# A transformer layer on eight cores: x transposed on the host and read with plain loads, its row-order copy cast by a separate DMA

## The chip, the cores and the metric

One Trainium2 chip, all eight cores. Each core runs the same program on one batch element of the input (4096 rows of 1024), so no core talks to another. The time is device microseconds of the slowest core. The kernel before takes 2436.91 us, the median of three runs.

## What is computed

The reference, cut to what matters, for one batch element:

```python
qkv = x @ W_qkv + b_qkv                       # x: [4096, 1024]
q, k, v = jnp.split(qkv, 3, axis=-1)
attn = jax.nn.softmax(q @ k.T / 32, axis=-1)
h = _layernorm(x + (attn @ v) @ W_out + b_out)
# feed-forward: groups of 16 rows, 64 expert slots; each slot takes one row of each group
perm = (logits == logits.max(over the 16 rows))
inter = relu(sel @ f1 + bias) @ f2
y = _layernorm(h + scatter(inter, perm))
```

x is needed twice: with its 1024 features on the partitions, as the moving operand of the projections, and in row order, as the residual that is added after the attention.

## The kernel before, in words

It is written engine by engine: a helper records an instruction for one engine (line 116 for every DMA, 121 for every wait, 127 and 130 for matmuls, 137 and 139 for ACT and DVE), and every wait is written by hand. The order of the program text is the order on each engine. Semaphores are counted per channel; a DMA adds 16 to its channel when it has landed.

Start. The GpSimd queue (POOL, queue q0 of the profile) casts DRAM to DRAM and DRAM to SBUF in this order: x rows 0 to 511 into the bf16 scratch xbf (channel xq0), the eight 128-row slabs of the Q weights (wc0 to wc7), x rows 512 to 1023 (xq1), eight slabs of K weights, x rows 1024 to 2047 (xq2), eight slabs of V weights, x rows 2048 to 4095 (xq3). All these 28 DMAs are issued at once; nothing waits on POOL.

Projections (Q, K, V). Eight blocks b of 512 rows. SyncE (SP, queue q1) waits for the piece of x that holds the block and for block b-2 to be done (two buffers), then issues eight transposing DMAs that put the block, features on partitions, into arena A. TensorE waits for all eight. Then, in order of the block: Q, eight groups m of eight 128x512 matmuls, banks m%4; K, the same; V, eight groups, banks 4 to 7. ScalarE (ACT) takes each Q group out of PSUM into one of two 512-column slots of the tile qstage and issues its DMA to the DRAM scratch qsp on its own queue (q10). Before it writes a slot it waits until the former DMA out of that slot, that of group m-2, has landed. The K groups also pass through ACT, into arena B; the V groups through VectorE (DVE), into arena C. The wait for the slot stands on ACT, in order, so K's evictions stand behind it; a bank of Q or K is free once ACT has taken it out, and V stands behind K on TensorE.

```python
wait("sync", xq_chan(b), 16)
wait("sync", "sT", xblk_T[buf])
for c in range(NCH):
    xv = dma("sync", xchan, A[:, xoff + c * 512: xoff + (c + 1) * 512],
             xbf_d[b * 512:(b + 1) * 512, c * 128:(c + 1) * 128],
             transpose=True)
```

```python
slot = m % 2
qchan = "qs%d" % slot
wait("scalar", qchan, P_cnt[qchan])      # the former write out of this slot
```

Attention. When the last projection is done, POOL loads the output weights and casts f1 and f2 (16 MB of fp32 each) DRAM to DRAM into bf16 scratch, eight DMAs in a row. SP loads the first two tiles of Q from qsp and, per 256 rows of queries, two 128-row tiles of xbf as the residual. Sixteen query tiles follow, each with 32 key tiles; then the routing logits, the gather of the selected rows, the expert matmuls, and the scatter with the second normalization. None of these stages is touched, but for the first load of the residual.

Of the kernel before, what the change touches and what calls it, by code (L numbers as in the profile page):

```python
# [8 lines left out]
F32 = mybir.dt.float32  # L9
BF16 = mybir.dt.bfloat16  # L10
# [3 lines left out]
D = 1024  # L14
# [7 lines left out]
def build_nc(S=4096, debug_scratch=False, stop_phase=99):  # L22
    nc = bass.Bass("TRN2", target_bir_lowering=False)
# [9 lines left out]
    SCR = "ExternalOutput" if debug_scratch else "Internal"  # L33

    x_d = nc.dram_tensor("x", [S, D], F32, kind="ExternalInput").ap()
    wqkv_d = nc.dram_tensor("wqkv", [D, 3 * D], F32, kind="ExternalInput").ap()
    bqkv_pc_d = nc.dram_tensor("bqkv_pc", [128, 16], F32, kind="ExternalInput").ap()
    bv_t_d = nc.dram_tensor("bv_t", [128, D], F32, kind="ExternalInput").ap()
# [10 lines left out]
    y_d = nc.dram_tensor("y", [S, D], F32, kind="ExternalOutput").ap()  # L49

    xbf_d = nc.dram_tensor("xbf", [S, D], BF16, kind=SCR).ap()
    qsp_d = nc.dram_tensor("qsp", [NCH, 128, S], BF16, kind=SCR).ap()
    hsp_d = nc.dram_tensor("hsp", [S, D], BF16, kind=SCR).ap()
    intersp_d = nc.dram_tensor("intersp", [ES, G, D], BF16, kind=SCR).ap()
# [23 lines left out]
          for i in range(8)]  # L78
# [27 lines left out]
    P_cnt = {s: 0 for s in CHANNELS + ["sT", "sV", "sC"]}  # L106
    P_ops = {e: [] for e in ENGINES}
    sems = {}
# [1 line left out]
    def op(eng, fn):  # L110
        P_ops[eng].append(fn)

    def dma(eng, chan, dst, src, **kw):
        P_cnt[chan] += 16
        op(eng, lambda e, d=dst, s=src, kw=kw, sm=chan:
           e.dma_start(d, s, **kw).then_inc(sems[sm], 16))  # L116
        return P_cnt[chan]

    def wait(eng, sname, v):
        if v and v > 0:  # L120
            op(eng, lambda e, sm=sname, vv=v: e.wait_ge(sems[sm], vv))

    def t_mm(out, lhsT, rhs, start, stop, inc=False):
        if inc:
            P_cnt["sT"] += 1
            op("tensor", lambda e, o=out, l=lhsT, r=rhs, st=start, sp=stop:
               e.matmul(o, l, r, start=st, stop=sp).then_inc(sems["sT"], 1))  # L127
        else:
            op("tensor", lambda e, o=out, l=lhsT, r=rhs, st=start, sp=stop:
               e.matmul(o, l, r, start=st, stop=sp))  # L130
        return P_cnt["sT"]
# [10 lines left out]
    def v_op(method, *args, inc=False, **kw):  # L142
        return eng_op("vector", "sV", method, *args, inc=inc, **kw)

    def c_op(method, *args, inc=False, **kw):
        return eng_op("scalar", "sC", method, *args, inc=inc, **kw)
# [20 lines left out]
    def xq_chan(b):  # L167
        row = b * 512
        for lo, hi, ch in xpieces:
            if lo <= row < hi:  # L170
                return ch
        return xpieces[-1][2]

    def emit_xpiece(i):
        if i < len(xpieces):
            lo, hi, ch = xpieces[i]
            dma("gpsimd", ch, xbf_d[lo:hi, :], x_d[lo:hi, :])

    emit_xpiece(0)
    for pi, (koff, pref) in enumerate(((0, "wc"), (1024, "wck"), (2048, "wcv"))):  # L180
        for k in range(NCH):
            dma("gpsimd", "%s%d" % (pref, k),
                A[:, k * 3072 + koff: k * 3072 + koff + 1024],
                wqkv_d[k * 128:(k + 1) * 128, koff:koff + 1024])
        emit_xpiece(pi + 1)
    dma("sync", "sm", BQ[:], bqkv_pc_d)
    dma("sync", "sm", GLM[:], glmask_d)
    dma("sync", "sm", IDT[:], ident_d)
# [10 lines left out]
    for b in range(NB):  # L199
        buf = b % 2  # L200
        xoff = XB0 + buf * 4096
        xchan = "xa%d" % buf
        wait("sync", xq_chan(b), 16)
        wait("sync", "sT", xblk_T[buf])
        xv = 0
        for c in range(NCH):
            xv = dma("sync", xchan, A[:, xoff + c * 512: xoff + (c + 1) * 512],
                     xbf_d[b * 512:(b + 1) * 512, c * 128:(c + 1) * 128],
                     transpose=True)

        wait("tensor", xchan, xv)

        for kind in ("Q", "K"):
            koff = 0 if kind == "Q" else 1024
            for m in range(NCH):
                pbi = m % 4
                sem, val = bank_free[pbi]
                wait("tensor", sem, val)
                tv = 0
                for k in range(NCH):  # L220
                    if b == 0 and m == 0:
                        wait("tensor",
                             ("wc%d" if kind == "Q" else "wck%d") % k, 16)
                    lhsT = A[:, k * 3072 + koff + m * 128:
                             k * 3072 + koff + m * 128 + 128]
                    rhs = A[:, xoff + k * 512: xoff + (k + 1) * 512]
                    tv = t_mm(pb[pbi][:], lhsT, rhs, k == 0, k == NCH - 1,
                              inc=(k == NCH - 1))
                wait("scalar", "sT", tv)
                wait("scalar", "sm", sm_done)  # L230
                if kind == "Q":
                    slot = m % 2
                    qchan = "qs%d" % slot
                    wait("scalar", qchan, P_cnt[qchan])
                    qsl = QS[:, slot * 512: slot * 512 + 512]
                    cv = c_op("activation", qsl, pb[pbi][:], AF.Identity,
                              inc=True, bias=BQ[:, m:m + 1])
                    wait("scalar", "sC", cv)
                    dma("scalar", qchan, qsp_d[m, :, b * 512:(b + 1) * 512], qsl)
                else:  # L240
                    cv = c_op("activation",
                              B[:, m * S + b * 512: m * S + (b + 1) * 512],
                              pb[pbi][:], AF.Identity, inc=True,
                              bias=BQ[:, 8 + m:8 + m + 1])
                bank_free[pbi] = ("sC", cv)

        wait("vector", "sV", init_v)
        wait("vector", "sm", sm_done)
        for sub in range(4):
            tt = b * 4 + sub  # L250
            for half in range(2):
                pbi = 4 + (sub * 2 + half) % 4
                sem, val = bank_free[pbi]
                wait("tensor", sem, val)
                tv = 0
                for k in range(NCH):
                    if b == 0 and sub == 0 and half == 0:
                        wait("tensor", "wcv%d" % k, 16)
                    lhsT = A[:, xoff + k * 512 + sub * 128:
                             xoff + k * 512 + sub * 128 + 128]  # L260
                    rhs = A[:, k * 3072 + 2048 + half * 512:
                            k * 3072 + 2048 + (half + 1) * 512]
                    tv = t_mm(pb[pbi][:], lhsT, rhs, k == 0, k == NCH - 1,
                              inc=(k == NCH - 1))
                wait("vector", "sT", tv)
                vv = v_op("tensor_tensor",
                          C_[:, tt * 1024 + half * 512: tt * 1024 + (half + 1) * 512],
                          pb[pbi][:], FP[:, half * 512:(half + 1) * 512],
                          ALU.add, inc=True)
                bank_free[pbi] = ("sV", vv)  # L270
        xblk_T[buf] = P_cnt["sT"]
# [48 lines left out]
    for qt in range(NQ):  # L320
# [6 lines left out]
            wait("tensor", sem, val)  # L327

        xrl_t = [0, 0]
        for sub in range(2):  # L330
            tt = qt * 2 + sub
            slot = tt % 2
            wait("sync", "sT", xres_free[slot])
            wait("sync", "h%d" % slot, h_spill[slot])
            xrl_t[slot] = dma("sync", "xr%d" % slot,
                              A[:, 15360 + slot * 1024: 15360 + (slot + 1) * 1024],
                              xbf_d[tt * 128:(tt + 1) * 128, :])
# [193 lines left out]
        while (ha_next + 1) * QC <= (qt + 1) * 256:  # L531
# [3 lines left out]
            for c in range(3):  # L535
# [3 lines left out]
                    transpose=True)  # L539
# [125 lines left out]
    for ec in range(4):  # L665
# [4 lines left out]
        for t in range(NT):  # L670
# [8 lines left out]
            for c in range(NCH):  # L679
                pbi = b0 + c // 4  # L680
                qtr = c % 4
                if qtr == 0:
# [8 lines left out]
                                                   c=NCH, e=16)  # L691
# [203 lines left out]
    for t in range(NT):  # L895
# [12 lines left out]
        for half in range(2):  # L908
            for c in range(4):
# [7 lines left out]
                      False, True, inc=True)  # L917
# [80 lines left out]
```

## Time and profile before

| | us |
|---|---|
| median of three runs | 2436.91 (2436.21 to 2487.02) |
| the profiled execution, its own time | 2434.68 |
| its span, slowest core (core 7) | 2433.1 |
| spans of the eight cores | 2405.8 to 2433.1 |
| TensorE busy in the span | 1932.8 |
| DMA bytes moved in the span | 230.62 MB |

The profile is of core 7. Its own time of 2434.68 us is 1.6 us above the span; the difference lies outside the first and the last instruction. In what follows, times on the axis are microseconds from the span's start. The DMA rows name queues: q0 is the one that POOL issues to, q1 that of SP, q10 that of ACT. A packet is the profile's unit, one contiguous run that one of the core's 16 DMA engines moves. Bytes of a cast are counted by its output.

### The profile page before, as it was taken

The page shows a single profiled execution, that of the slowest core. Times are in us where ns is not written, and L with a number is a line of the kernel's source. Part 1 is how long each engine was busy: PE and PEld are TensorE (multiplying, and loading weights), DVE is VectorE, ACT ScalarE, POOL GpSimd, SP SyncE. Part 2 cuts the span into 40 slices and gives each one's busy share as a digit, 9 for nine tenths or more (in the row PEclk, how much of TensorE's full clock was granted, in tenths as well). Part 3 has the DMA queues.
Part 4 walks back from the last instruction along what each step waited for, and adds up shares of the span by engine and source line. Part 5 has one row for each costly group of instructions (what it writes and reads, how often), then busy time and mean ns, then how long its engine had stood idle before and what let it go on. Part 6 is the DMA issues. An engine that isn't in the chain of part 4 may idle for free.

```text
span 2433.1 us, 36001 instructions; the slowest of 8 cores (2405.8 to 2433.1 us)
## 1 busy us (share of the span) xinstructions
PE 1932.8 (79%) x13216; PEld 1301.7 (54%) x13216; DVE 517.1 (21%) x840; ACT 555.9 (23%) x1121; POOL 127.4 (5%) x241
## 2 busy tenths in 40 slices
PE   0089999999399999999999999993567677665565
PEld 0034444478288777778877777881334343332222
DVE  0000101110110111111011111001514333432555
ACT  0023232222022222222222222220244333331000
POOL 2000000100000000000000000000011111112110
PEclk9999999999699999999999999996655655565777
DMA  9932131399600100001000100006265556556996
GB/s 131 120 62 61 38 67 44 71 116 115 107 10 18 40 27 27 27 19 31 19 27 27 40 27 23 6 19 136 70 176 183 165 181 170 175 164 196 314 311 234
DMA packets 234759, 230.62 MB, mean 95 GB/s; under 512 B 147488, under 2 KB 172064, under 8 KB 233760
## 3 DMA queue, kind: packets, MB, share of 16 engines
q0 software_dynamic: 21968, 84.03, 17.6%
q1 hardware_dynamic: 117904, 85.55, 13.9%
q10 hardware_dynamic: 94720, 58.74, 8.6%
q8 instruction: 114, 1.87, 0.3%
q14 instruction: 53, 0.43, 0.1%
HBM read 178.06 MB, written 92.27 MB: 111 GB/s over the span
## 4 chain that ended last, share of the span: by engine, by line
PE 63%; DMA 17%; another core or an unknown queue 7%; DVE 5%; issue 3%; ACT 2%; SPq 1%; DVEq 1%; ACTq 0%; POOL 0%; POOLq 0%
PE pb L130 55%; DMA intersp<-arenaB 8%; PE pb L127 8%; DMA arenaC<-hsp 4%; DMA arenaB<-intersp 2%; DMA y<-arenaF 2%; SPq L116 1%; DVE arenaB L137 1%; ACT arenaB L137 1%; DVE arenaA L137 1%; DMA arenaB<-f1b 1%; DVE bnbuf L139 1%; DVEq L139 1%; DVE arenaA L139 1%
## 5 line engine op out<-in xcount | busy, mean ns | idle before, releaser
L130 PE MATMUL pb<-arenaA,arenaB 128*128 128x256 bf16 (+1 forms) x4032 | 580.6, 288 | 63.6 <-DMA arenaA<-qsp 43.5
L130 PE MATMUL pb<-arenaA 128*128 128x512 bf16 x1856 | 457.7, 381 | 135.5 <-DMA arenaA<-xbf 133.0
L130 PE MATMUL pb<-arenaA,arenaC 128*128 128x256 bf16 x4120 | 540.0, 274 | 27.3 <-DVE arenaA L137 19.0
L130 PEld LDWEIGHTS pb<-arenaA,arenaB 128*128 128x128 bf16 (+1 forms) x4032 | 414.9, 105 | 170.2 <-issue 116.3
L130 PEld LDWEIGHTS pb<-arenaA,arenaC 128*128 128x128 bf16 x4120 | 402.3, 98 | 82.0 <-issue 34.7
L137 ACT ACTIVATE arenaA<-pb,smalls 128x256 bf16<-128x256 f32 x512 | 241.3, 474 | 796.7 <-PE pb L127 763.2
L130 PEld LDWEIGHTS pb<-arenaA 128*128 128x128 bf16 x1856 | 179.3, 98 | 364.8 <-issue 171.0
L130 PE MATMUL pb<-arenaB 128*128 128x512 bf16 (+1 forms) x384 | 164.1, 518 | 153.5 <-DVE arenaB L137 76.7
L139 DVE RECIPROCAL arenaF<-pb 128x256 f32<-128x256 f32 x16 | 28.1, 1758 | 881.8 <-PE pb L127 881.8
L130 PEld LDWEIGHTS pb<-arenaB 128*128 128x128 bf16 (+1 forms) x384 | 40.7, 112 | 266.6 <-issue 255.0
L127 PE MATMUL pb<-arenaA,arenaB 128*128 128x256 bf16 (+1 forms) x576 | 165.9, 288 | 0.0
L137 DVE CAST arenaB<-pb 128x512 bf16<-128x512 f32 x128 | 88.5, 692 | 272.5 <-DMA intersp<-arenaB 162.5
L130 PE MATMUL pb<-arenaC 128*128 128x128 bf16 x896 | 101.1, 282 | 51.8 <-DMA arenaC<-hsp 25.4
L127 PE MATMUL pb<-arenaA,ones_t 128*128 128x256 bf16 x512 | 139.6, 273 | 0.0
L137 DVE TENSOR_TENSOR arenaC<-pb,arenaF 128x512 bf16<-128x512 f32 x64 | 44.3, 692 | 422.2 <-PE pb L127 422.2
L130 PEld LDWEIGHTS pb<-arenaC 128*128 128x128 bf16 x896 | 79.1, 127 | 72.6 <-issue 71.7
L137 ACT ACTIVATE arenaB<-pb 128x512 bf16<-128x512 f32 x128 | 75.7, 596 | 161.3 <-DMA intersp<-arenaB 137.2
L139 DVE BATCH_NORM_STATS2 bnbuf<-pb 128x6 f32<-128x512 f32 x128 | 86.2, 694 | 112.5 <-PE pb L127 107.8
L116 POOL DMA_DIRECT2D intersp<-arenaB x128 | 69.2, 541 | 497.5 <-ACT arenaB L137 340.1
L139 ACT ACTIVATE bnbuf<-bnbuf,smalls 128x1 f32<-128x1 f32 x64 | 18.8, 294 | 327.2 <-DVE bnbuf L137 316.1
L137 ACT ACTIVATE arenaA<-pb 128x512 bf16<-128x512 f32 x128 | 76.4, 598 | 58.4 <-PE pb L127 58.1
L137 ACT ACTIVATE qstage<-pb,s_bqkv_pc 128x512 bf16<-128x512 f32 x64 | 44.0, 688 | 171.2 <-PE pb L127 125.9
(54 smaller groups left out, 944.6 us busy)
## 6 DMA issues: line engine op xcount, KB each, us to landing
arenaC<-hsp SPq DMA_DIRECT2D x128, 256.0 KB, 3.6
intersp<-arenaB POOLq DMA_DIRECT2D x128, 256.0 KB, 3.2
arenaB<-intersp SPq DMA_DIRECT2D x64, 256.0 KB, 16.3
arenaB<-intersp POOLq DMA_DIRECT2D x64, 256.0 KB, 9.2
y<-arenaF ACTq DMA_DIRECT2D x32, 512.0 KB, 9.6
qsp<-qstage ACTq DMA_DIRECT2D x64, 128.0 KB, 2.4
arenaA<-qsp SPq DMA_DIRECT2D x16, 512.0 KB, 3.9
arenaA<-xbf SPq DMA_DIRECT2D x32, 256.0 KB, 2.6
```

Of the source, the lines that this page charges most:

```text
L116: e.dma_start(d, s, **kw).then_inc(sems[sm], 16))
L127: e.matmul(o, l, r, start=st, stop=sp).then_inc(sems["sT"], 1))
L130: e.matmul(o, l, r, start=st, stop=sp))
L137: getattr(e, m)(*a, **k).then_inc(sems[sname], 1))
L139: op(eng, lambda e, a=args, k=kw, m=method: getattr(e, m)(*a, **k))
```

## The change

The host now also passes xt, the transpose of x, as a second fp32 input. The four pieces that POOL casts at the start are columns of xt, into a new scratch xbft, in place of rows of x into xbf. SP's 64 transposing DMAs become 64 plain DMAs of 128 rows by 512 columns out of xbft. xbf is still needed for the residual: one more DMA on POOL's queue, after the fourth piece, casts the whole of x, on a channel of its own (xbc), and SP waits for it ahead of the first residual load.

```diff
@@ emit_xpiece
             lo, hi, ch = xpieces[i]
-            dma("gpsimd", ch, xbf_d[lo:hi, :], x_d[lo:hi, :])
+            dma("gpsimd", ch, xbft_d[:, lo:hi], xt_d[:, lo:hi])
@@ start
         emit_xpiece(pi + 1)
+    xbc_done = dma("gpsimd", "xbc", xbf_d[:, :], x_d[:, :])
@@ projections, block b
             xv = dma("sync", xchan, A[:, xoff + c * 512: xoff + (c + 1) * 512],
-                     xbf_d[b * 512:(b + 1) * 512, c * 128:(c + 1) * 128],
-                     transpose=True)
+                     xbft_d[c * 128:(c + 1) * 128, b * 512:(b + 1) * 512])
@@ attention, query tile qt
         xrl_t = [0, 0]
+        if qt == 0:
+            wait("sync", "xbc", xbc_done)
@@ host
         m["x"] = np.ascontiguousarray(x[b])
+        m["xt"] = np.ascontiguousarray(x[b].T)
```

The queue of POOL at the start of the program, before. A DMA's shape is that of its destination in runs: 32x16384 is 32 contiguous runs of 16384 bf16 elements, 32 KB each.

```order
L116 DMA xbf<-x 32x16384
L116 DMA arenaA<-wqkv 128x1024 x8
L116 DMA xbf<-x 32x16384
L116 DMA arenaA<-wqkv 128x1024 x8
L116 DMA xbf<-x 64x16384
L116 DMA arenaA<-wqkv 128x1024 x8
L116 DMA xbf<-x 128x16384
L116 DMA arenaA<-wout 128x1024 [waits sT]
```

The same place in the changed program:

```order
L118 DMA xbft<-xt 1024x512
L118 DMA arenaA<-wqkv 128x1024 x8
L118 DMA xbft<-xt 1024x512
L118 DMA arenaA<-wqkv 128x1024 x8
L118 DMA xbft<-xt 1024x1024
L118 DMA arenaA<-wqkv 128x1024 x8
L118 DMA xbft<-xt 1024x2048
L118 DMA xbf<-x 256x16384
L118 DMA arenaA<-wout 128x1024 [waits sT]
```

The four pieces are now 1024 runs each, of 1, 1, 2 and 4 KB, and a DMA of 256 runs of 32 KB stands behind them. All else on the queue keeps its place.

SP's queue at the blocks 0 to 2, before:

```order
L116 DMA_TRANSPOSE arenaA<-xbf 128x512 [waits xq0]
L116 DMA_TRANSPOSE arenaA<-xbf 128x512 x7
L116 DMA_TRANSPOSE arenaA<-xbf 128x512 [waits xq1]
L116 DMA_TRANSPOSE arenaA<-xbf 128x512 x7
L116 DMA_TRANSPOSE arenaA<-xbf 128x512 [waits xq2,sT]
L116 DMA_TRANSPOSE arenaA<-xbf 128x512 x7
```

And in the changed program:

```order
L118 DMA arenaA<-xbft 128x512 [waits xq0]
L118 DMA arenaA<-xbft 128x512 x7
L118 DMA arenaA<-xbft 128x512 [waits xq1]
L118 DMA arenaA<-xbft 128x512 x7
L118 DMA arenaA<-xbft 128x512 [waits xq2,sT]
L118 DMA arenaA<-xbft 128x512 x7
```

The waits stay, the transposes become plain loads of 128 runs of 1 KB. ACT's queue is not changed; at the start it reads, the wait for the slot standing from the third group on:

```order
L137 ACTIVATE qstage<-pb,s_bqkv_pc 128x512 [waits sT,sm]
L116 DMA qsp<-qstage 128x512 [waits sC]
L137 ACTIVATE qstage<-pb,s_bqkv_pc 128x512 [waits sT,sm]
L116 DMA qsp<-qstage 128x512 [waits sC]
L137 ACTIVATE qstage<-pb,s_bqkv_pc 128x512 [waits sT,sm,qs0]
L116 DMA qsp<-qstage 128x512 [waits sC]
L137 ACTIVATE qstage<-pb,s_bqkv_pc 128x512 [waits sT,sm,qs1]
L116 DMA qsp<-qstage 128x512 [waits sC]
```

## Rows read from the trace of the kernel before

**Rows 1.** Groups of instructions, 0 to 467 us; busy, mean, idle before and releaser

```profile
L130 PE MATMUL pb<-arenaA 128*128 128x512 bf16 x1344 | 323.7, 381 | 133.0 <-DMA arenaA<-xbf 133.0
```

**Rows 2.** Timeline, 0 to 480 us: start, length, engine, what, idle before

```profile
15.82 123.98 SPq L116 DMA_TRANSPOSE arenaA<-xbf  x16
...
132.97 3.15 PE L130 MATMUL pb<-arenaA 128*128 128x512 bf16 x7 [132.97 <-DMA arenaA<-xbf]
...
136.33 2.47 PE L130 MATMUL pb<-arenaA 128*128 128x512 bf16 x7
...
138.85 1.67 PE L130 MATMUL pb<-arenaA 128*128 128x512 bf16 x7
...
466.70 0.38 PE L127 MATMUL pb<-arenaA 128*128 128x512 bf16 x1
```

**Rows 3.** Busy time by stretch: TensorE through one block, granted clock, DMA share

```profile
175.00:216.00 41.00, 41.00 (x192) 18.61 (x190) 5.53 (x8) 10.99 (x16) 0.00 (x0) 1.00 0.22 52
```

**Rows 4.** DMA issues of 0 to 17 us: KB each, us from issue to landing

```profile
xbf<-x POOLq DMA_DIRECT2D x1, 1024.0 KB, 14.2
...
arenaA<-wqkv POOLq DMA_DIRECT2D x8, 256.0 KB, 73.6
...
xbf<-x POOLq DMA_DIRECT2D x1, 4096.0 KB, 116.0
```

**Rows 5.** DMA queues, 44 to 52 us (packets, MB, share of 16 engines): weights against transposes

```profile
q0 software_dynamic: 588, 1.07, 91.5%
q1 hardware_dynamic: 588, 0.14, 14.9%
```

**Rows 6.** DMA queues, 100 to 120 us: the last piece of x against transposes

```profile
q0 software_dynamic: 65, 2.13, 92.0%
q1 hardware_dynamic: 68, 0.01, 0.6%
```

**Rows 7.** DMA queues, 105 to 115 us

```profile
q0 software_dynamic: 35, 1.15, 100.0%
```

**Rows 8.** DMA queues, 120 to 450 us: q10 carries the 64 writes of Q

```profile
q10 hardware_dynamic: 9216, 8.39, 9.3%
```

**Rows 9.** DMA queues, 540 to 620 us: the casts of f1 and f2 against plain DMAs

```profile
q0 software_dynamic: 322, 8.45, 96.4%
q10 hardware_dynamic: 258, 0.50, 1.6%
q1 hardware_dynamic: 306, 0.16, 1.3%
```

**Rows 10.** DMA issues of 500 to 620 us: the plain load of a Q tile

```profile
arenaA<-qsp SPq DMA_DIRECT2D x1, 512.0 KB, 108.9
```

**Rows 11.** DMA issues of 547 to 549 us: one write of ACT

```profile
hsp<-arenaA ACTq DMA_DIRECT2D x1, 256.0 KB, 43.4
```

**Rows 12.** Timeline of TensorE, 644 to 648 us

```profile
646.54 1.65 PE L130 MATMUL pb<-arenaA,arenaB 128*128 128x256 bf16 x7 [37.57 <-DMA arenaA<-qsp]
```

**Rows 13.** Timeline of ACT, 139 to 150 us: the wait for a slot of qstage

```profile
141.15 0.69 ACT L137 ACTIVATE qstage<-pb,s_bqkv_pc 128x512 bf16<-128x512 f32 x1 [1.21 <-DMA qsp<-qstage]
```

**Rows 14.** DMA queues, 1640 to 1680 us: 1024 runs of 128 bytes of the controller's cast

```profile
q0 software_dynamic: 1040, 0.13, 5.1%
```

**Rows 15.** Spans and granted clock of single cores

```profile
core 6: 2405.8 us, clock 0.877
core 7: 2433.1 us, clock 0.873
```

More of the change, by code:

```diff
@@ L35, in build_nc @@
     x_d = nc.dram_tensor("x", [S, D], F32, kind="ExternalInput").ap()
+    xt_d = nc.dram_tensor("xt", [D, S], F32, kind="ExternalInput").ap()
     wqkv_d = nc.dram_tensor("wqkv", [D, 3 * D], F32, kind="ExternalInput").ap()
@@ L51, in build_nc @@
     xbf_d = nc.dram_tensor("xbf", [S, D], BF16, kind=SCR).ap()
+    xbft_d = nc.dram_tensor("xbft", [D, S], BF16, kind=SCR).ap()
     qsp_d = nc.dram_tensor("qsp", [NCH, 128, S], BF16, kind=SCR).ap()
```

2 rows, old and new, of the table CHANNELS are left out of this document.

## The prediction

> **What bounds the kernel now.** I read the groups of instructions of the first 467 us, then the timeline around TensorE's first matmul, then the DMA queues stretch by stretch. TensorE's first matmul starts at 132.97 us, and the whole idle time is put down to the transposed loads of block 0 [rows 1, 2]. From there TensorE is never idle until the last projection at 467.1 us (466.70 + 0.38). In a clean block its 192 matmuls take 41.0 us by the window, and a group of eight starts every 1.72 us, so 24 groups are 41.3 us [rows 2, 3]. The granted clock is 1.00 there, that is 2.4 GHz.
>
> Why does block 0 arrive at 133 us when its piece of x has landed at 1.6 + 14.2 = 15.8 us [rows 4]? The queues tell it. From 44 to 52 us q0 moves 588 packets and q1 588; from 100 to 120 us, where q0's packets are 32 KB, 65 against 68 [rows 5, 6]. So the 16 DMA engines take one packet of q0 and one of q1 in turn, whatever their size. A packet of 32 KB takes 20 x 16 x 0.92 / 65 = 4.5 us, and each small packet of another queue waits for one. The transposes thus end with the last cast of x, which lands at 15.8 + 116.0 = 131.8 us [rows 4]. The same thing is seen later: from 540 to 620 us q0 casts f1 and f2 in 32 KB packets, 8.45 MB in 80 us; a plain load of 512 KB takes 108.9 us, a single ACT write 43.4 us, and TensorE stands idle for 37.57 us for that load [rows 9 to 12]. Plain DMAs starve as transposes do.
>
> Everything after 467 us (1966 us of the span) keeps its instructions, and its own flood of f1 and f2 starts with it. I cost it at no change. So the sum is about when the eighth block ends.
>
> **Removed: the transposes.** A plain load of 128 runs of 1 KB is 9 packets per engine, as the writes of Q show: 9216 / 64 / 16 = 9, the ninth being the semaphore's [rows 8]. A block is 8 x 8 = 64 data packets per engine. Beside the Q weights (2 KB packets, 0.915 x 8 x 16 / 588 = 0.20 us each [rows 5]) plus some 0.06 us for q1's own, 64 turns are about 17 us. Piece 0 lands near 16 us as before, so block 0 is there at about 33 us, and the Q weights with it. TensorE starts 100 us earlier. Alone this would be a gain of up to 100 us, less what the K and V weights hold back.
>
> **What is late next: the weights.** q0 goes in order. The V weights land about at 13.3 + 73.6 = 86.9 us for the median of the eight [rows 4]; the last one about 92 us, where the fourth piece must begin (4.19 MB at 2.13 MB per 20 us are 39 us before its landing at 131.8 [rows 4, 6]). I leave this as it is, since the bytes ahead of them are the same; transposes no longer take turns, but loads and writes do. Block 0 does Q and K meanwhile, waits, and ends its V part at 92 + 8 x 1.72 + 2 = about 108 us. Then SP may issue the load of block 2, and TensorE begins block 1, whose load has landed long before.
>
> **Added: the cast of the whole of x.** In the trace 8.45 MB in 32 KB packets take 80 us, and 1.15 MB 10 us, so 8.39 MB are 73 to 79 us [rows 7, 9]; I take 76. It stands behind the fourth piece, which I leave at 132 us (64 packets of 4 KB per engine at (132 - 92) / 64 = 0.6 us). So the new DMA runs from 132 to 208 us, with 256 / 16 = 16 packets per engine, 4.7 us each. During it every other queue gets 16 packets per engine, and no more. Before, q0 was empty from 132 us on, and the writes of Q had the DMA engines to themselves.
>
> **What that does to the writes of Q.** ACT waits for the write of group m-2 before it takes out group m, already now a little (1.21 us) [rows 13]. All writes share q10's ring, 9 packets per engine each. The last Q group of block 1 (m = 7) needs write 5, that is 6 x 9 = 54 packets. From 108 to 132 us a turn is 0.6 us of q0 plus some 0.1 for the others: 24 / 0.7 = 34 packets. Then 16 more until 208 us. That is 50, so write 5 lands right after 208 us. Behind it stand on ACT the evictions of K, and behind K on TensorE the V part. Four K banks are open meanwhile, so groups K3 to K7 and V remain: 0.7 + 13 x 1.72 = 23 us, with the landing 24. Block 1 ends at 232 us. A restart after a long idle costs about 3 us more (the first two groups took 3.15 and 2.47 us, against 1.67 [rows 2]); I keep that for the range.
>
> **What that does to the load of block 2.** It needs 64 packets per engine; 34 + 16 come through by 208 us, the other 14 within 2 us after it. Hidden behind the writes, but only just.
>
> **The sum.** Six blocks remain: 232 + 6 x 41.3 = 480 us, against 467.1 now: +13 us. 2434.7 + 13 = 2448 us. The profiled execution is 2.2 us under the median of the runs; I don't correct for it. The wait for xbc at the first residual load costs nothing: the cast has landed 250 us before. The break-even is a block 1 that ends (or a block 2 whose load lands) at 467.1 - 248 = 219 us.
>
> Unknown: casts DRAM to DRAM in small runs. 1024 runs of 128 bytes cost 0.051 x 40 x 16 / 1040 = 31 ns each [rows 14]; from the other side a packet of weights of 2 KB costs 0.20 us against 4.5 / 16 = 0.28 us for the same bytes in a 32 KB packet. So the four pieces (256 packets per engine, 64 more than weights) may take up to 256 x 0.031 = 8 us longer, or up to a third less of the 79 us (-25 us). I take nothing, the value between, and keep both.
>
> **Rivals.**
> B, only the load of block 2 is late: faster. If the V weights land 6 us earlier or a turn is cheaper, Q of block 1 has 30 / 0.7 = 43 packets before the big ones; write 5 then lands at 132 + 11 x 4.7 = 184 us, block 1 ends at 208, and block 2 starts at 200 to 210. The time is 2434.7 - (219 - 205) = 2421 us, 2413 at the least. For it: the margin is 4 to 12 packets. Against it: the 16 engines do not end together (0.92 busy, last landings late), and a write lands with its slowest engine.
>
> C, nothing starves. If a turn of another queue carried several packets, block 0 would end at 108 us and seven blocks follow: 108 + 7 x 41.3 = 397 us, 70 us less, 2365 us. The trace speaks against it: 306 packets of q1 and 258 of q10 to 322 of q0 [rows 9]. The Trainium skill, "DMA: Bandwidth & Descriptors", section on queues, rings and completion order, would have it so: an engine drains a whole packet of 9 to 17 descriptors from one ring before it switches. By that rule a write of Q would need one turn, and rival C would stand. This case's trace shows turns of one packet of the profile, so I give it little.
>
> D, slower by over 2%. Casting columns of xt with short rows at a 16 KB pitch might run at half the byte rate: the pieces then take 79 us longer, the V weights 40, and the big cast ends near 290 us. Block 1 would end at about 314 us, +95 us, 2530 us. It decides from a fourth piece that lands after 170 us. No row shows such a pattern; the 31 ns per run speak against a halving.
>
> E, moderately slow small runs (the +8 us above, the restart, and slowest engines late by some 5 to 20 us more): +20 to +45 us, 2465 us.
>
> That the change doesn't do what it says: if x's piece 0 were the limit at the start, TensorE would still start near 130 us. Its landing at 15.8 us excludes it.
>
> **How the numbers follow.** The forecast (backlog of Q writes, 2435 to 2456 us) 0.49, B 0.25, C 0.07, D 0.05, E 0.14. Core 7 sets the time, and core 6 is 27 us shorter [rows 15]; an uneven shift of cores stays within the forecast's own range. The range of 8 in 10 takes in the forecast, nearly all of B and half of E: 2411 to 2466 us. Over 2% (about what a measurement of this kernel can tell from no change) is 49 us: faster than that is C, 0.07; slower is D, 0.05; the rest, 0.88, lies within.
>
> **What would show it.** Right: TensorE's first matmul near 33 us, a gap before V of block 0 until about 90 us; then ACT's waits for qsp writes summing to 60 to 90 us in block 1, with write times of 40 us and more; the cast of x landing at 200 to 212 us; q0 and q10 at equal packets there. Wrong: block 2 starting before 200 us (B or C), a fourth piece landing far from 132 us (D, E), or TensorE idle in a block after the third.

## The result, and the profile after

The change makes the kernel slower: 2471.82 us, median of 8 runs, against 2437.59 us for the kernel before; the ratio is 1.0143, 95% interval 1.0121 to 1.0165. That is 34 us. Each of the two medians takes in one run in which the cores of one die showed a lower granted clock; the ratio, and all ratios and times below, leave such runs out. The forecast was 2448 us with a range up to 2466 us: right in sign and in place, too small in size.

The profiled execution of the changed kernel took 2468.92 us, the span of its slowest core, again core 7, 2467.3 us. First the page's group of the projection matmuls (busy, mean ns, then the idle time before them with what ended most of it), which answers to [rows 1]. It covers the whole run, so its count takes in 512 matmuls of later stages:

```profile
L132 PE MATMUL pb<-arenaA 128*128 128x512 bf16 x1856 | 469.7, 389 | 154.1 <-ACT qstage L139 102.6
```

The idle time has changed its name. Before it was one wait of 133.0 us for the transposed loads; now 46.3 us go to the plain loads of block 0, and 102.6 us end with ACT's eviction of Q into qstage. What ACT itself waits for is in the waits of 0 to 480 us (total, times, longest):

```profile
ACT qstage L139 <- DMA qsp<-qstage: 152.7, 27, 49.2
```

The timeline of ACT shows each of these (start, length, engine, what; in brackets the idle time before and its releaser). Block 0, then block 1:

```profile
61.52 0.69 ACT L139 ACTIVATE qstage<-pb,s_bqkv_pc 128x512 bf16<-128x512 f32 x1 [8.24 <-DMA qsp<-qstage]
75.01 0.69 ACT L139 ACTIVATE qstage<-pb,s_bqkv_pc 128x512 bf16<-128x512 f32 x1 [9.89 <-DMA qsp<-qstage]
...
125.06 0.69 ACT L139 ACTIVATE qstage<-pb,s_bqkv_pc 128x512 bf16<-128x512 f32 x1 [21.41 <-PE pb L129]
126.78 0.69 ACT L139 ACTIVATE qstage<-pb,s_bqkv_pc 128x512 bf16<-128x512 f32 x1 [1.04 <-PE pb L129]
176.69 0.69 ACT L139 ACTIVATE qstage<-pb,s_bqkv_pc 128x512 bf16<-128x512 f32 x1 [49.22 <-DMA qsp<-qstage]
211.55 0.69 ACT L139 ACTIVATE qstage<-pb,s_bqkv_pc 128x512 bf16<-128x512 f32 x1 [34.17 <-DMA qsp<-qstage]
222.54 0.69 ACT L139 ACTIVATE qstage<-pb,s_bqkv_pc 128x512 bf16<-128x512 f32 x1 [10.30 <-DMA qsp<-qstage]
225.94 0.69 ACT L139 ACTIVATE qstage<-pb,s_bqkv_pc 128x512 bf16<-128x512 f32 x1 [2.72 <-DMA qsp<-qstage]
```

Block 1 starts its Q part at about 124 us, evicts two groups at once, and then two groups in 85 us. The whole cast of x is what runs meanwhile: issued at 17.2 us, it landed at 17.2 + 207.8 = 225.0 us, behind a fourth piece that landed at 16.5 + 136.7 = 153.2 us. "Behind" is by order of issue: the 16 engines do not keep step. On core 7 the first engine began a 32 KB packet of the cast at 129.4 us, and 45 of its 256 packets had begun by 153.2 us; on the eight cores the first began at 127.5 to 130.3 us. The DMA issues (KB each, us to landing), answering to [rows 4]:

```profile
xbf<-x POOLq DMA_DIRECT2D x1, 8192.0 KB, 207.8
xbft<-xt POOLq DMA_DIRECT2D x1, 4096.0 KB, 136.7
```

The first two writes of Q in block 1, issued in 125 to 127 us and in 127 to 128 us:

```profile
qsp<-qstage ACTq DMA_DIRECT2D x1, 128.0 KB, 50.8
qsp<-qstage ACTq DMA_DIRECT2D x1, 128.0 KB, 83.9
```

And the queues from 160 to 200 us (packets, MB, share of 16 engines), answering to [rows 6, 9]:

```profile
q0 software_dynamic: 131, 4.29, 98.8%
q1 hardware_dynamic: 130, 0.12, 1.4%
q10 hardware_dynamic: 85, 0.08, 0.6%
```

131 packets of 32 KB against 130 of 1 KB: one in turn, as forecast. Equal counts alone would also fit longer bursts on both sides, nine against nine; but from 155 to 200 us no stretch of 0.7 us holds more than five starts of q1's 1 KB packets, over all 16 engines together. q10's 85 are 5 per engine in 40 us, and a write needs 9. The forecast had q10 at as many packets as q0; it had fewer, since with two slots at most two writes are under way.

TensorE does start early, and then stands. Its timeline (columns as above), with the restart at 46.31 us in place of 132.97 us [rows 2]:

```profile
46.31 3.14 PE L132 MATMUL pb<-arenaA 128*128 128x512 bf16 x7 [46.31 <-DMA arenaA<-xbft]
...
89.53 3.15 PE L132 MATMUL pb<-arenaA 128*128 128x512 bf16 x7 [5.64 <-ACT qstage L139]
...
106.88 0.38 PE L132 MATMUL pb<-arenaA 128*128 128x512 bf16 x1 [2.31 <-DMA arenaA<-wqkv]
...
177.53 3.12 PE L132 MATMUL pb<-arenaA 128*128 128x512 bf16 x7 [44.04 <-ACT qstage L139]
212.38 3.15 PE L132 MATMUL pb<-arenaA 128*128 128x512 bf16 x7 [31.53 <-ACT qstage L139]
223.37 3.14 PE L132 MATMUL pb<-arenaA 128*128 128x512 bf16 x7 [7.41 <-ACT qstage L139]
```

The stretches 160 to 200 us and 240 to 280 us (length; busy and count of TensorE, weight loads, DVE, ACT, POOL; granted clock; DMA share; GB/s), to be read beside [rows 3]:

```profile
160.00:200.00 40.00, 3.33 (x8) 1.02 (x8) 0.00 (x0) 0.69 (x1) 0.00 (x0) 0.54 1.01 112
240.00:280.00 40.00, 40.00 (x187) 18.15 (x186) 5.53 (x8) 10.61 (x16) 0.00 (x0) 1.00 0.17 53
```

One group of eight matmuls in 40 us, with the DMA engines full; then a clean block, at 2.4 GHz again. The last projection ends at 502.2 us (501.82 + 0.38), 35.1 us later than before, and the span is 34.2 us longer. So the whole loss lies ahead of the attention.

For the experiments one number serves best: the end of the projections, which is when POOL issues the first load of the output weights. The median over the eight cores is 463.7 us before and 502.3 us after.

| kernel | end of projections, us (median of cores) | time against the kernel before |
|---|---|---|
| before | 463.7 | 1 |
| after | 502.3 | 1.0143 (1.0121 to 1.0165) |
| e1, cast of x in 2 KB packets | 467.4 | 0.9999 (0.9975 to 1.0022) |
| e2, six slots for Q | 486.4 | 1.0073 (1.0047 to 1.0099) |
| e3, before, x in 2 KB packets | 466.0 | 0.9979 (0.9965 to 0.9993) |
| e4, contiguous pieces | 529.8 | two runs, 2506.9 and 2510.3 us, against 2447.1 us |
| e5, e1 and e2 together | 431.3 | 0.9836 (0.9816 to 0.9855) |
| e6, and f1, f2 in 2 KB packets | 431.1 | 0.967 (0.9602 to 0.9737) |
| e7, before with all three edits | 443.3 | 0.971 (0.9675 to 0.9746) |
| e8, cast of x after the projections | 422.9 | 1.019 (1.0167 to 1.0213) |
| e9, loads gated by the fourth piece | 546.4 | one run, 2525.9 us against 2448.7 us |
| e10, e6 with the cast at block 5 | 429.3 | 0.9644 (0.9621 to 0.9667) |
| e11, before, transposes gated | 469.4 | one run, 2432.4 us against 2427.1 us |
| e12, e6 with the V weights earlier | 416.2 | 0.9604 (0.9574 to 0.9633) |

The ratios are to the kernel before on the same chip; it took 2427.1 to 2448.7 us on the chips of the experiments, so times of different rows are compared by their ratios.

### The profile page after: what moved, and what is told of

Its sections match the earlier page's. It is cut to its first block, busy times and chain, and to the rows that moved or that the text cites. A ratio compares the mean times of both kernels' runs of the same rounds, so it can differ in the third digit from the quotient of the medians.

```text
span 2467.3 us, 36004 instructions; the slowest of 8 cores (2432.8 to 2467.3 us)
## 1 busy us (share of the span) xinstructions
PE 1949.8 (79%) x13216; PEld 1303.8 (53%) x13216; DVE 516.5 (21%) x840; ACT 554.4 (22%) x1121; POOL 129.0 (5%) x242
## 4 chain that ended last, share of the span: by engine, by line
PE 62%; DMA 21%; DVE 5%; another core or an unknown queue 4%; issue 3%; ACT 1%; SPq 1%; DVEq 1%; ACTq 0%; POOL 0%; POOLq 0%
PE pb L132 54%; PE pb L129 8%; DMA intersp<-arenaB 7%; DMA y<-arenaF 4%; DMA arenaC<-hsp 4%; DMA qsp<-qstage 3%; SPq L118 1%; DVE arenaB L139 1%; DMA arenaA<-xbft 1%; DVE arenaA L139 1%; DMA xbft<-xt 1%; DMA arenaB<-f1b 1%; DVE bnbuf L141 1%; DVEq L141 1%
## 5 line engine op out<-in xcount | busy, mean ns | idle before, releaser
L132 PE MATMUL pb<-arenaA 128*128 128x512 bf16 x1856 | 469.7, 389 | 154.1 <-ACT qstage L139 102.6
## 6 DMA issues: line engine op xcount, KB each, us to landing
xbf<-x POOLq DMA_DIRECT2D x1, 8192.0 KB, 207.8
```

## The experiments

**e1: the length of the turn.** Even and odd rows of x as two DMAs cannot be merged into long runs:

```diff
-    xbc_done = dma("gpsimd", "xbc", xbf_d[:, :], x_d[:, :])
+    xsp = x_d.rearrange("(r two) d -> two r d", two=2)
+    xbsp = xbf_d.rearrange("(r two) d -> two r d", two=2)
+    for hh in range(2):
+        xbc_done = dma("gpsimd", "xbc", xbsp[hh], xsp[hh])
```

> The changed kernel with one edit: the cast of the whole of x is cut into packets of 2 KB (even rows, then odd rows) in place of 256 packets of 32 KB; same bytes, same place on POOL's queue. Theory (a queue's turn is one packet, so the long packets starve the others): a turn shrinks from 4.7 us to about 0.3 us, the writes of Q of block 1 take some 4 us instead of 35 to 50 us, block 1 ends near 180 us instead of 254 us, and the last projection near 444 us instead of 502 us: about 2412 us. Rival (the DMA engines or the HBM are simply full, whatever the packets' size): writes stay at 35 us and more while the cast runs, and the time stays at 2465 to 2475 us.

The projections end 35 us earlier, at 467 us, and the whole loss is gone. The cast was slower for it. On this run's core 5 the first half, issued at 17.2 us, took 184.4 us, and the median of the two is 202.5 us, so the second took 220.6 us and landed at about 238 us; on core 5 of the changed kernel the cast landed at 223.8 us:

```profile
xbf<-x POOLq DMA_DIRECT2D x1, 4096.0 KB, 184.4
xbf<-x POOLq DMA_DIRECT2D x2, 4096.0 KB, 202.5
```

So the engines were full for longer, and the writes still came through sooner: the rival, full engines whatever the packets' size, falls. But the gain is three fifths of the 58 us expected; ACT still waited 123.2 us in all in the first 700 us:

```profile
ACT qstage L139 <- DMA qsp<-qstage: 123.2, 32, 15.0
```

The longest wait fell from 49.2 to 15.0 us, and there are more of them. In block 1 most waits are 5 to 8 us, and the writes took 12.7 to 14.8 us each, where 4 us was expected. From 140 to 180 us q0 moved 1658 packets, a turn of 40 x 16 / 1658 = 0.39 us, and nine such turns are 3.5 us. So counting turns does not give the time of a write beside short packets; what takes the other 10 us is not shown.

**e2: the wait for the slot.** The cast keeps its 32 KB packets, ACT gets six slots:

```diff
-                    slot = m % 2
+                    slot = (b * 8 + m) % 6
...
-                    qsl = QS[:, slot * 512: slot * 512 + 512]
+                    if slot < 2:
+                        qsl = QS[:, slot * 512: slot * 512 + 512]
+                    else:
+                        qsl = FP[:, 1024:2048].bitcast(BF16)[:, (slot - 2) * 512: (slot - 1) * 512]
```

> The changed kernel with six slots for the evicted Q instead of two (four of them in the unused upper half of the fp32 tile arenaF; its later load then waits for the writes of Q). The cast of x keeps its 32 KB packets. Theory (ACT's wait for a slot is what TensorE stands behind in block 1): the eviction of group 7 then needs write 1 and not write 5; with write 1 landing at about 211 us as in the changed kernel block 1 ends at 235 us at the latest instead of 254 us, and block 2 can't start before its load lands at about 227 us: the last projection ends at 475 to 483 us instead of 502 us, 2440 to 2450 us. Rival (the load of block 2 ends last, the writes are beside the path): block 2 starts at 254 us as before, 2465 to 2475 us.

16 us earlier by the median of the cores (486.4 us), and 0.7% where the change alone is 1.4%. The wait for the slot is on the path. TensorE still stood 38.33 and 31.13 us, now for an eviction into the new slots:

```profile
180.77 3.14 PE L132 MATMUL pb<-arenaA 128*128 128x512 bf16 x7 [38.33 <-ACT arenaF L139]
215.48 3.15 PE L132 MATMUL pb<-arenaA 128*128 128x512 bf16 x7 [31.13 <-ACT arenaF L139]
```

Six slots do not carry over eight groups when a write takes 35 us.

**e3: the same turn in the kernel before.** Each piece of x as even and odd rows, transposes kept, two slots:

```diff
-            dma("gpsimd", ch, xbf_d[lo:hi, :], x_d[lo:hi, :])
+            for hh in range(2):
+                xqd[ch] = dma("gpsimd", ch,
+                    xbf_d[lo:hi, :].rearrange("(r two) d -> two r d", two=2)[hh],
+                    x_d[lo:hi, :].rearrange("(r two) d -> two r d", two=2)[hh])
...
-        wait("sync", xq_chan(b), 16)
+        wait("sync", xq_chan(b), 32)
```

> The kernel before with one edit: the four pieces of x are cast in packets of 2 KB (each piece as even and odd rows), transposes kept. Theory (turns by packet): block 0's transposes need 8 x 34 = 272 turns of 0.3 us each, some 80 us from 16 us on, so TensorE starts near 95 us instead of 133 us, and the last projection ends at 430 to 440 us: 2400 to 2410 us. Rival (transposes are slow beside any full DMA queue): TensorE starts at 130 us or later, 2435 us or more.

A miss that taught the most. TensorE starts at 102.91 us, as the theory of turns says, 24.5 us earlier than the same core did before (127.4 us). Yet the projections end at 466.0 us, no earlier than before. Of these 24.5 us, 21.8 us went into four waits of TensorE for an eviction of Q, two of them in these lines:

```profile
102.91 3.14 PE L130 MATMUL pb<-arenaA 128*128 128x512 bf16 x7 [102.91 <-DMA arenaA<-xbf]
124.81 3.14 PE L130 MATMUL pb<-arenaA 128*128 128x512 bf16 x7 [8.95 <-ACT qstage L137]
132.22 3.12 PE L130 MATMUL pb<-arenaA 128*128 128x512 bf16 x7 [3.84 <-ACT qstage L137]
```

So this early start was worth nothing: while POOL's queue is full and ACT has two slots, the Q part runs at the pace of the writes. It is no rule for every early start: e8, below, also has two slots and starts some 80 us earlier than the kernel before, and keeps half of that.

**e4: long packets for the pieces.** The host lays xt out piece by piece, so each piece is contiguous and cast in 32 KB packets:

```diff
-            dma("gpsimd", ch, xbft_d[:, lo:hi], xt_d[:, lo:hi])
+            dma("gpsimd", ch,
+                xbft_d[lo * D:hi * D].rearrange("(p w) -> p w", p=D),
+                xt_d[lo * D:hi * D].rearrange("(p w) -> p w", p=D))
```

> The changed kernel with the transposed input laid out piece by piece on the host, so that each of the four pieces is one contiguous block and is cast in packets of 32 KB again, as before the change. Theory 1 (the casts in short runs at a 16 KB pitch cost the 21 us by which the fourth piece lands later, 153 us against 132 us): the fourth piece lands at about 132 to 137 us, the cast of x at 205 to 210 us, and as the writes of Q get few turns, block 1 ends at about 240 us: 2450 to 2458 us. Theory 2 (the pieces are late since plain loads and writes take turns with them): the fourth piece stays near 150 us, and the time at 2465 us or more.

The fourth piece landed at 139 to 142 us on the eight cores, between the two theories, against 142 to 153 us in the changed kernel. The time was a clear miss: 2506.9 us. I had left out that block 0's writes now met 32 KB packets too. TensorE stood before the third piece was through:

```profile
84.78 3.14 PE L132 MATMUL pb<-arenaA 128*128 128x512 bf16 x7 [21.89 <-ACT qstage L139]
127.11 3.14 PE L132 MATMUL pb<-arenaA 128*128 128x512 bf16 x7 [36.79 <-ACT qstage L139]
170.82 3.15 PE L132 MATMUL pb<-arenaA 128*128 128x512 bf16 x7 [40.15 <-ACT qstage L139]
```

The short runs of the transposed pieces, a side effect of the change, had kept the loss of the projections' end at 39 us (502.3 against 463.7) instead of 66.

**e5: both edits.**

> The changed kernel with both edits: the cast of x in 2 KB packets and six slots for the evicted Q. Theory (the two together take away what TensorE stands behind: the length of a turn and the wait for a slot): block 0 ends at about 118 us, held by the V weights alone, and then seven blocks run without a gap, 118 + 7 x 41.4 = 408 us; with some waits left 410 to 425 us instead of 502 us, 2355 to 2375 us. Rival (each edit takes away the same wait, so the gains don't add): the end of the projections stays at 460 to 470 us as with the 2 KB packets alone, 2435 us or more.

They add up and more: 35 us and 16 us alone, 71 us together (431.3 us). The rival falls. The expected 410 to 425 us are missed, since TensorE still waits 23.3 us for weights and 14.4 us for evictions, with the DMA engines full until the cast lands.

**e6: the casts of f1 and f2.**

```diff
-        fc1_done = dma("gpsimd", "fc1", f1b_d[i * 256:(i + 1) * 256, :],
-                       f1_d[i * 256:(i + 1) * 256, :])
+        fc1_done = dma("gpsimd", "fc1", f1b_d[:, i * 1024:(i + 1) * 1024],
+                       f1_d[:, i * 1024:(i + 1) * 1024])
...
+    f2s = f2_d.rearrange("e (j two w) -> two e j w", two=2, w=1024)
+    f2bs = f2b_d.rearrange("e (j two w) -> two e j w", two=2, w=1024)
+    for i in range(2):
+        for hh in range(2):
+            fc2_done = dma("gpsimd", "fc2", f2bs[hh, i * 32:(i + 1) * 32],
+                           f2s[hh, i * 32:(i + 1) * 32])
```

> As the run before, and the casts of f1 and f2 at the start of the attention are also made in 2 KB packets. Theory (TensorE's idle time of 37 us ahead of the third query tile comes from turns of 32 KB): that wait falls to under 5 us, some 35 to 40 us less than the run before, 2315 to 2340 us. Rival (the load of the query tile is slow since the DMA engines are full): the wait stays above 25 us.

The projections end where they did, and the median falls from 2405.0 to 2359.5 us. TensorE's waits for a tile of Q in the first 760 us, e5 and then e6:

```profile
PE pb L132 <- DMA arenaA<-qsp: 46.5, 2, 40.3
```

```profile
PE pb L132 <- DMA arenaA<-qsp: 5.6, 1, 5.6
```

This confirms the reading of [rows 9 to 12]: the wait of 37.57 us before the change was of the same kind.

**e7: is the transposed input worth anything?** The kernel before with the edits of e3, e2 and e6.

> The kernel before, transposes kept, with the same three edits: all casts of x and of f1 and f2 in 2 KB packets, six slots. It tells what the transposed input is worth once nothing starves. TensorE starts at 103 us as in the run with the pieces in 2 KB packets; if the slots hide the writes, eight blocks of 41.4 us follow: 434 us, against 467 us, and 37 us less in the attention: 2360 to 2375 us, some 25 to 35 us above the version with the transposed input. Rival (the transposed input is worth nothing): the two come out equal within 10 us.

0.971 against 0.967, intervals overlapping, medians 13 us apart. With short turns and six slots the transposing DMAs do nearly as well: TensorE starts at 102.29 us, 56 us after e6, and ends its projections 12 us later. The expected 25 to 35 us are missed, the rival's 10 us nearly met.

**e8: the cast behind the projections.**

With xsp and xbsp as in e1:

```diff
-    xbc_done = dma("gpsimd", "xbc", xbf_d[:, :], x_d[:, :])
...
     wout_done = P_cnt["wo"]
+    for hh in range(2):
+        xbc_done = dma("gpsimd", "xbc", xbsp[hh], xsp[hh])
```

> The changed kernel with the cast of the whole of x moved behind the projections (after the load of the output weights, ahead of the casts of f1 and f2), in 2 KB packets; two slots as in the changed kernel. Theory (of the 35 us lost, the cast of x makes all, and the small packets of the pieces give the rest its pace): block 0 is as it was (end at 123 us), the Q part of block 1 is slow until the fourth piece lands near 150 us, then nothing waits: the last projection ends at 430 to 445 us, and with up to 20 us of wait for the residual the time is 2405 to 2430 us. Rival (late pieces and the turns of block 0 make the loss, not the cast): the last projection ends at 480 us or later.

The projections end at 422.9 us: 79 us before the changed kernel and 41 before the kernel before. The 79 us are the price of the cast where the change puts it, and the 41 us what the transposed input would bring without it. The total was a miss, 1.019. I had allowed 20 us for the residual, and TensorE waited 87.16 us for it:

```profile
582.76 3.42 PE L132 MATMUL pb<-arenaA 128*128 128x512 bf16 x8 [87.16 <-DMA arenaA<-xbf]
```

SP issued the two residual loads at 536.57 us, when the cast had landed. Beside the 32 KB packets of f1 and f2 TensorE had the one that it needed 46 us later; the median of the two is 63.1 us from issue to landing.

**e9 and e11: why the pieces were late.** One edit in either kernel keeps the loads of the blocks, and with them the writes of Q, off the DMA engines until the fourth piece has landed:

```diff
-        wait("sync", xq_chan(b), 16)
+        wait("sync", "xq3", 16)
```

> The changed kernel with one edit that is meant to be slow: SP waits for the fourth piece before it loads any block, so that no load of a block and no write of Q takes a turn while the four pieces and the weights are cast. It asks why the fourth piece lands at 141 to 153 us in the changed kernel and at 122 to 135 us before. If the short runs of the pieces cost it themselves, it lands at 145 us or later here too. If the loads and writes that now get their turns cost it, it lands at 120 to 135 us. Some of both: 135 to 145 us. TensorE starts at that time, and as the writes of Q meet the cast of x from then on, the last projection ends at about 540 to 560 us, 2500 to 2525 us.

> The kernel before with the same edit as the changed kernel had in the run with gated loads: SP waits for the fourth piece of x before it issues any transpose, so the casts have the DMA engines to themselves, in 32 KB packets for x. In the changed kernel the fourth piece landed at 130 to 133 us under this edit. If short runs cost nothing by themselves, it lands at 126 to 133 us here too. If they cost something, it lands earlier here by that much: 115 to 122 us means some 10 to 15 us for 8 MB. Block 0's transposes then begin at that time and take about 10 us without competition, and eight blocks of 41.8 us follow: the last projection at 460 to 475 us, 2430 to 2445 us.

The fourth piece of e9, in short runs, issued at 16.5 us, took 113.1 to 116.3 us: it landed at 130 to 133 us. That of e11, in 32 KB packets, issued at 15.7 us, took 104.1 to 105.1 us: it landed at 120 to 121 us. One core of each:

```profile
xbft<-xt POOLq DMA_DIRECT2D x1, 4096.0 KB, 114.6
```

```profile
xbf<-x POOLq DMA_DIRECT2D x1, 4096.0 KB, 104.9
```

So short runs cost 10 to 11 us by themselves for the 8 MB. The two runs were on different chips, on which the kernel before differs by 0.9%, so a little of this may be the chip. In the changed kernel the fourth piece landed at 142 to 153 us, a median over the cores of 149.2 us against 131.4 us in e9. Turns of the loads and writes make most of these 18 us: in e8, which has them but no cast behind, it landed at 141.6 to 146.4 us, median 144.4. The last 5 us or so go with the cast of x behind the piece. These runs were on different chips too, and how a cast behind would delay the slower engines is not shown. e11 shows one thing more: with transposes that start only at 120 us, the projections end at 469.4 us, 6 us later than before. The kernel before gets next to nothing from issuing its transposes early.

**e10: the cast where the slots can hide it.** POOL waits for block 4 ahead of the cast of x, and the rest is e6.

> The version with all casts but the weights in packets of 2 KB or less and with six slots, and the cast of x issued when block 4 is done. The cast then falls beside blocks 5 and 6, far from the loads of the weights, and the six slots hide its turns from TensorE. Theory: the gaps of blocks 1 and 2 go, the last projection ends at 410 to 418 us instead of 425 to 437 us, and the residual's first load, 70 us later, finds the cast landed: 2335 to 2350 us. Rival (the cast costs the same wherever it lies): 2355 to 2365 us.

0.9644 against 0.967, within the intervals. The projections end at 429.3 us. The gaps of block 1 and 2 shrink, but the stretch beside the cast, 320 to 360 us, has TensorE busy for 33.4 of 40 us. The rival was right: the cast costs about the same in these two places.

**e12: the V weights ahead of the third piece.**

```diff
-        emit_xpiece(pi + 1)
+        if pi == 0:
+            emit_xpiece(1)
+    emit_xpiece(2)
+    emit_xpiece(3)
```

> The best version so far (all casts but the weights in packets of 2 KB or less, six slots, the cast of x behind the fourth piece), with the third piece of x cast after the V weights instead of ahead of them. In the version before, TensorE waits for the V weights until 110 us, though it was through with K near 83 us. Theory: the V weights land some 15 us earlier, at 90 to 95 us, block 0 ends at about 104 us instead of 118 us, and the last projection comes 10 to 15 us earlier, at 415 to 422 us in place of 431 us: 2342 to 2350 us. Rival (the same bytes are moved by then, and the gap only moves into the blocks 1 and 2): within 4 us of the version before, 2355 to 2363 us.

The best version by its median ratio: 2333.5 us, 0.9604 of the kernel before (0.9574 to 0.9633). The interval overlaps those of e6 and e10; what sets it apart is the end of the projections, 15 us ahead of e6's 431.1 us. The wait for the V weights in block 0 has nearly gone.

## Why the prediction was right and wrong

**The mechanism.** "So the 16 DMA engines take one packet of q0 and one of q1 in turn" held between q0 and q1 to the packet, 131 to 130. That the writes of Q would take the place of the transposes as the thing waited for held too, and so did the place: block 1, from the cast's start to its end, with write 5 landing right behind it. e1, e2 and e8 show each part of it: short turns take 35 us off, more slots 16, no cast 79.

**The count of turns, and some luck.** The 34 + 16 turns by which I placed write 5 did not happen. They take the writes as queued up, and with two slots only two are under way. By that count the 29 us from block 0's end to the fourth piece's landing would have carried 29 / 0.7 = 41 packets per engine, over four writes. In fact the first two were issued then and neither had landed. I also took the engines as in step: an engine that begins the cast at 129.4 us passes nine packets of a write in nine turns of 4.7 us, by 172 us, and the first write landed at about 176 us. The place came out right because the writes left over went through in 1.8 us each once the cast was out, so that block 1 hangs on the cast's end and hardly on the count.

**Rival C** and the Trainium skill's account of whole packets of 9 to 17 descriptors in a turn ("DMA: Bandwidth & Descriptors", queues, rings and completion order) did not come about for these DMAs. The first two writes of block 1 took 50.8 and 83.9 us, and q1's packets came without bursts of nine. Nor does that account lead to rival C, as I had it: it would hold for q0 as well, and nine of its 32 KB packets keep an engine for 9 x 4.7 = 42 us (an estimate from this case's packets).

**The terms of the sum.** By core 7:

| term | forecast | measured |
|---|---|---|
| TensorE starts | 33 | 46.3 |
| V weights landed | 92 | about 109 |
| block 0 ends | 108 | 123 to 124 |
| fourth piece lands | 132 | 153.2 |
| from there to the landing of the cast of x | 76 | 71.8 |
| from the cast's end to the end of block 1 | 24 | 28.7 |
| block 1 ends | 232 | 253.7 |
| six blocks | 248 | 248.5 |
| the rest of the span | 1966 | 1965.1 |

(The end of block 1 is read back from the first eviction of block 2, at 255.49 us, less the one group of 1.72 us ahead of it.) The step that failed is one sentence: "I leave this as it is, since the bytes ahead of them are the same; transposes no longer take turns, but loads and writes do", and with it the fourth piece "which I leave at 132 us". It was left at 132 us and measured 153.2 us. That is 21 of the 22 us by which block 1 ended later than forecast, if one goes from landing to landing; the rest is 4 us less to the cast's landing and 5 us more behind it. Since the cast had begun on some engines at 129 us, the two landings share their time: the fourth piece and the cast together were done at 225.0 us against 208, 17 us late, and the tail adds 5. The tail holds the restart of about 3 us that I had kept for the range: the group at 223.37 us ran at half speed, 3.14 us against 1.67.

Why the sentence failed, by e8, e9 and e11: short runs cost 10 to 11 us, more than the 8 us of my upper bound; the cast behind the piece goes with some 5 us; and turns given to others are not free. Those of the loads and writes cost 13 us (e8 against e9, medians), those of the transposes before 7 us (127.3 us against 120.4 us of e11). From 60 to 75 us q1 took 25.4% of the DMA engines for 678 packets, 15 x 16 x 0.254 / 678 = 0.09 us each, where I had 0.06:

```profile
q0 software_dynamic: 675, 1.34, 68.3%
q1 hardware_dynamic: 678, 0.62, 25.4%
q10 hardware_dynamic: 369, 0.34, 7.4%
```

A transpose's small packet costs a third of that (0.149 x 8 x 16 / 588 = 0.03 us [rows 5]). Block 0's load took longer than forecast too: piece 0 landed at 1.6 + 16.9 = 18.5 us, and TensorE started 28 us later, not 17. Still, the plain loads did come through earlier than the transposes, and paid for it with q0's time, on which the weights and every later piece depend.

**The writes in block 0.** I had TensorE through with Q and K long before the V weights. In fact ACT waited 2 to 10 us for a slot from the third group on, and K was done at 104 us, just as the weights came. It cost nothing here, since both ended together, but it is what ate the gain in e3.

**The range.** Case E had the right size, +20 to +45 us, and the right kind, late pieces and the restart, at a chance of 0.14. The range took in only half of it. The bounds of the unknown cost were set from the runs' own price and not from what turns take.

## What to carry to other kernels

When a DMA is taken off the start, ask which queue is full there, how long its packets are, and which small transfer an engine waits for in order: with 32 KB packets in one queue a write of nine packets per engine took 45 to 84 us here, and starting the engine earlier only moves the wait. Cut bulk casts into short runs (an even and an odd half is enough), give the producer enough slots to ride over a slow write, and put what is needed first first. With the transposed input they gave 4.0% here; without it, and without the reordering, 2.9% (e7). The transposed input, which was the change, has little of that: 0.4% between e6 and e7, inside the intervals.

## What the runs showed that I had not expected

Cutting an 8 MB cast from 32 KB to 2 KB packets slowed the cast and sped up the kernel. In e1 POOL's queue was through at 235 to 241 us on the eight cores, as against 218 to 225 us in the changed kernel, and the projections ended 35 us earlier all the same. A busy queue may end later and cost less, if what others wait for gets its turns.

With the engines nearly to itself the queue was even: in e11 the fourth piece landed within 1.0 us on all eight cores. In the kernel before, with transposes taking turns, the same piece landed between 122 and 135 us, and the spread of the cores' spans follows it in part.
